# Weighting the fetched expert rows on ScalarE and adding them on VectorE in two instructions

## The reference

```python
def collect(eo, i, p, pr):
    sel = eo[i, p]                                  # two rows of 128 for each token
    return jnp.sum(pr[..., None] * sel, axis=1)     # weighted by the token's two shares
return jax.vmap(collect)(o, idx, pos, probs)
...
x = x + gb * _L1_ffn_ref(h, ...)
```

## Time and profile before

| | |
|---|---|
| median of 3 runs | 2884.38 us (2880.81 to 2885.79) |
| the profiled execution | 2883.22 us, its span 2882.0 us |
| instructions | 33776 |
| PE busy | 2172.6 us, 75% |
| DVE busy | 2227.5 us, 77% |
| ACT busy | 1554.3 us, 54% |
| POOL busy | 1204.0 us, 42% |
| TensorE's granted clock, mean | 0.878 of full |
| chain of waits, by engine | DVE 35%, PE 16%, issue 12%, ACT 9%, POOL 6% |

### The profile page before, as it was taken

The page is one execution under the profiler, slowest core; times in us unless marked ns, Lnnn a source line. Parts: engine busy times, 40 slices in busy tenths (PEclk is TensorE's granted clock), DMA queues, the critical chain, the costliest instruction groups (busy, mean ns, idle before and its releaser), DMA issues.

```text
span 2882.0 us, 33776 instructions
## 1 busy us (share of the span) xinstructions
PE 2172.6 (75%) x8767; PEld 1113.4 (39%) x8767; DVE 2227.5 (77%) x5937; ACT 1554.3 (54%) x3331; POOL 1204.0 (42%) x1166
## 2 busy tenths in 40 slices
PE   4159777988788777978878787878779787868654
PEld 2016222553244522644244522544235532444214
DVE  5874788968898688978799787978879786952371
ACT  4316824776176823885267823876157842744423
POOL 2020253715455153724555063723445154634461
PEclk7589799988998898989989899989989799989857
DMA  4001112232043312333133312323133221313223
GB/s 108 0 22 36 24 38 84 84 101 83 27 124 72 104 52 75 97 80 93 38 102 83 102 49 69 110 68 101 31 106 95 86 65 54 104 41 112 83 80 102
DMA packets 137461, 215.13 MB, mean 75 GB/s; under 512 B 17872, under 2 KB 57440, under 8 KB 134112
## 3 DMA queue, kind: packets, MB, share of 16 engines
q1 hardware_dynamic: 133088, 203.88, 25.0%
q0 software_dynamic: 4096, 8.40, 1.0%
HBM read 190.06 MB, written 22.15 MB: 74 GB/s over the span
## 4 chain that ended last, share of the span: by engine, by line
DVE 35%; PE 16%; issue 12%; ACT 9%; POOL 6%; DVEq 3%; DMA 2%; POOLq 0%; ACTq 0%; SPq 0%
DVE ps_rest L1644 6%; DVE wmask L833 6%; DVE best L975 4%; DVEq L977 3%; DVE hg L1656 3%; ACT wmask L815 3%; PE ps_rest L1385 2%; DVE z L1143 2%; POOL slots L1800 2%; PE ps_rest L1375 2%; PE ps_rest L1831 2%; PE ps_rest L1845 1%; PE ps_rest L1471 1%; DMA cols<-slots 1%; PE ps_rest L1833 1%
## 5 line engine op out<-in xcount | busy, mean ns | idle before, releaser
L1445 POOL TENSOR_TENSOR gat<-sil,cbs 128x512 f32<-128x512 f32 x256 | 325.1, 1274 | 469.8 <-ACT sil L1410 396.6
L1410 ACT ACTIVATE sil<-ps_rest,w_b1T 128x512 f32<-128x512 f32 x256 | 175.7, 686 | 471.5 <-PE ps_rest L1385 417.4
L833 DVE TENSOR_SCALAR_CACHE_REDUCE wmask<-z,tc 128x512 bf16<-128x512 f16 x512 | 349.2, 741 | 21.3 <-ACT z L800 18.1
L1009 POOL TENSOR_SCALAR wmask<-wmask 128x512 bf16<-128x512 bf16 x256 | 158.1, 617 | 341.7 <-DVE wmask L966 337.7
L1093 PE MATMUL ps_att<-z,Vp 128*32 128x128 f32 x2048 | 269.6, 277 | 16.8 <-DVE z L1165 16.8
L1385 PE MATMUL ps_rest<-rest_hT,WF 128*128 128x512 f32 x512 | 279.9, 633 | 0.0
L1375 PE MATMUL ps_rest<-gat,WP 128*128 128x512 f32 x512 | 268.7, 608 | 14.4 <-POOL gat L1445 14.4
L766 PE MATMUL ps_att<-qk 128*128 128x512 bf16 x512 | 222.6, 452 | 45.6 <-DMA qk<-bounce 21.6
L1093 PEld LDWEIGHTS ps_att<-z,Vp 128*32 128x32 f32 x2048 | 202.5, 110 | 131.3 <-issue 93.4
L1697 POOL TENSOR_TENSOR rest_c<-rest_c,hg 128x512 f32<-128x512 f32 x128 | 162.5, 1270 | 130.0 <-DVE hg L1656 129.9
L1684 POOL TENSOR_TENSOR gat<-cols,cbs 128x512 f32<-128x512 f32 x128 | 163.5, 1278 | 123.2 <-DVE cols L1565 123.2
(11 more groups left out here) (361 smaller groups left out, 4824.5 us busy)
## 6 DMA issues: line engine op xcount, KB each, us to landing
cbs<-spreads SPq DMA_DIRECT2D x128, 256.0 KB, 3.7
ccs<-spreads SPq DMA_DIRECT2D x128, 256.0 KB, 3.4
WF<-in_w SPq DMA_DIRECT2D x64, 256.0 KB, 2.7
WP<-in_w SPq DMA_DIRECT2D x64, 256.0 KB, 2.6
WF<-in_wfc SPq DMA_DIRECT2D x64, 256.0 KB, 2.7
WG<-in_wgate SPq DMA_DIRECT2D x64, 256.0 KB, 3.0
WP<-in_wproj SPq DMA_DIRECT2D x64, 256.0 KB, 3.0
qk<-bounce SPq DMA_DIRECT2D x32, 384.0 KB, 5.2
```

What stands on the lines that cost most here:

```text
L833: od.up(dve.tensor_scalar(wmask[:, i, :], z_at[i], tc[:, 0, i:i + 1], None, ALU.is_ge, ALU.add, accum_out=tc[:, 1, i:i + 1]))
L1445: weighed0.up(pool.tensor_tensor(gat[m % 2], sil[m % 2], cbs[e % 2][:], ALU.mult))
```

## The change

- `act_finish` is new: ScalarE waits for the eight fetches and for the shares, and multiplies each of the eight blocks of 128 columns of `back` by its share, in place (`ACT.Copy` with `scale` a per-partition operand). The fourth and the eighth count on a new semaphore, `shared_out`.
- `dve_finish` waits for `shared_out` twice and adds to `x` in two `tensor_tensor` instructions of 512 columns. Both count on `out1`, which has two counts per batch instead of four; between them VectorE waits for its own first.
- The planner has one thread more, `act_finishes`. The summed cost of `dve_finishes` goes from 4.96 to 1.44. All marks of all 29 threads have other values; `PERIOD` goes from -65.7 to 14.9 and `NEAR` from 0.152 to 0.243.

```diff
-PERIOD = -65.7
+PERIOD = 14.9
 TIMETABLE = {
...
-    "act_rest": (84.0600, (4864.9, 5034.0, 4871.5, 5557.9)),
+    "act_rest": (84.0600, (4455.4, 5292.9, 4111.4, 5412.5)),
...
-    "dve_finishes": (4.9600, (6158.0, 3649.8, 3263.1, 5364.1)),
+    "dve_finishes": (1.4400, (6874.3, 5480.6, 4086.7, 6120.0)),
...
+    "act_finishes": (3.6000, (7806.3, 3975.0, 3965.4, 6006.5)),
...
-    "act_attention": (76.8200, (9436.8, 7899.4, 8737.1, 13894.2)),
-    "dve_attention": (101.0400, (8189.2, 7002.3, 6134.6, 6121.7)),
+    "act_attention": (76.8200, (10505.4, 7134.6, 7634.1, 12822.5)),
+    "dve_attention": (101.0400, (8954.7, 6583.0, 5232.7, 6101.3)),
...
-    turned_back, added, out1 = sig("turned_back", 4), sig("added", 2), sig("out1", NT)
+    turned_back, added, out1 = sig("turned_back", 4), sig("added", 2), sig("out1", 2)
+    shared_out = sig("shared_out", 2)
...
     def dve_finish(b):
-        yield fetched.all(b)
-        dve.wait_ge(*fetched.all(b))
-        x = xr[b % 3]
-        for i, p in enumerate(("p1", "p2")):
-            for j in range(NT):
-                done = (od if i == 0 else out1).up(dve.scalar_tensor_tensor(x[:, j, :], back[:, i * NT + j, :], sv[p][:, j:j + 1], x[:, j, :],
-                                                                             ALU.mult, ALU.add))
-                yield 0.62
-            if i == 0:
-                od.settle()
+        x = xr[b % 3]
+        for i in range(2):
+            yield shared_out.at(b, i)
+            dve.wait_ge(*shared_out.at(b, i))
+            out1.up(dve.tensor_tensor(x[:], x[:], back[:, i * NT:(i + 1) * NT, :], ALU.add))
+            yield 0.72
+            if i == 0:
+                dve.wait_ge(*out1.at(b, 0))
+
+    def act_finish(b):
+        yield fetched.all(b)
+        act.wait_ge(*fetched.all(b))
+        yield shares.at(b)
+        act.wait_ge(*shares.at(b))
+        for i, p in enumerate(("p1", "p2")):
+            for j in range(NT):
+                done = act.activation(back[:, i * NT + j, :], back[:, i * NT + j, :], ACT.Copy, scale=sv[p][:, j:j + 1])
+                if j == NT - 1:
+                    shared_out.up(done)
+                else:
+                    oa.up(done)
+                yield 0.45
...
-    NEAR = 0.152
+    NEAR = 0.243
```

More of the change, by code:

```diff
@@ L46 @@
 FULL = (TOPK + 7) // 8
-PERIOD = -65.7
+PERIOD = 14.9
 TIMETABLE = {
-    "pe_rest": (155.6425, (4063.8, 2909.1, 2381.5, 1586.6)),
-    "act_rest": (84.0600, (4864.9, 5034.0, 4871.5, 5557.9)),
[L53 to L59, removed]
-    "dve_finishes": (4.9600, (6158.0, 3649.8, 3263.1, 5364.1)),
[L61 to L67, removed]
-    "act_attention": (76.8200, (9436.8, 7899.4, 8737.1, 13894.2)),
-    "dve_attention": (101.0400, (8189.2, 7002.3, 6134.6, 6121.7)),
[L70 to L79, removed]
@@ new lines @@
+    "pe_rest": (155.6425, (4417.8, 3623.9, 3606.2, 1766.5)),
+    "act_rest": (84.0600, (4455.4, 5292.9, 4111.4, 5412.5)),
+    "dve_rest": (96.6350, (3157.5, 6748.6, 6383.8, 4999.9)),
+    "pool_rest": (113.9225, (1737.4, 2015.9, 2844.8, 1657.8)),
+    "sp_rest": (15.3000, (7089.8, 5438.4, 6355.6, 6693.4)),
+    "pe_mixtures": (10.3100, (5846.9, 7611.3, 5250.0, 5587.3)),
+    "act_mixtures": (6.3000, (8134.6, 6365.4, 4720.0, 8578.6)),
+    "dve_mixtures": (13.5500, (5347.6, 5446.2, 5900.5, 6884.3)),
@@ new lines @@
+    "pool_mixtures": (3.9300, (8331.2, 9232.9, 12384.5, 14764.3)),
+    "dve_finishes": (1.4400, (6874.3, 5480.6, 4086.7, 6120.0)),
+    "pool_finishes": (9.0400, (3887.3, 6024.2, 5163.6, 5137.3)),
+    "act_finishes": (3.6000, (7806.3, 3975.0, 3965.4, 6006.5)),
+    "sp_finishes": (0.9000, (6856.1, 10708.9, 11455.7, 10402.6)),
+    "pe_choices": (42.2400, (1472.2, 1002.7, 2586.1, 2335.4)),
+    "act_choices": (2.5600, (10489.3, 11025.6, 11082.9, 4280.8)),
+    "dve_choices": (58.8100, (4745.6, 4518.9, 5384.4, 5070.8)),
@@ new lines @@
+    "pool_choices": (20.4800, (9372.4, 7538.3, 6851.4, 10027.2)),
+    "pe_attention": (57.4700, (7997.8, 5869.9, 5443.7, 5402.4)),
+    "act_attention": (76.8200, (10505.4, 7134.6, 7634.1, 12822.5)),
+    "dve_attention": (101.0400, (8954.7, 6583.0, 5232.7, 6101.3)),
+    "pool_attention": (6.5463, (6819.4, 6563.5, 6868.9, 8126.4)),
+    "sp_attention": (10.3500, (9501.8, 7012.5, 7718.2, 6678.1)),
+    "pe_prepares": (8.9150, (6494.4, 7059.7, 6925.8, 6588.7)),
+    "act_prepares": (3.9500, (4847.8, 5429.3, 4767.3, 0.0)),
@@ L80 @@
+    "dve_prepares": (13.8550, (11309.4, 12249.7, 11982.4, 11990.6)),
+    "pe_refills": (12.8000, (8692.6, 6412.3, 7360.2, 8369.5)),
+    "act_refills": (19.2000, (6209.8, 8412.5, 7473.7, 6238.0)),
+    "sp_rows": (0.3937, (9033.9, 8097.1, 6623.4, 7312.1)),
+    "sp_ups": (10.6875, (6668.4, 7321.3, 7935.9, 8230.1)),
+    "sp_downs": (7.0875, (7933.8, 6539.7, 5628.0, 3274.3)),
 }
@@ L2116, in dve_finishes, with act_finishes @@
             yield from dve_finish(b)
+    def act_finishes():
+        for b in every:
+            yield from act_finish(b)
     def pool_finishes():
@@ L2182, in emit @@
            ("act", "act_mixtures", act_mixtures()), ("dve", "dve_mixtures", dve_mixtures()), ("pool", "pool_mixtures", pool_mixtures()),
-           ("dve", "dve_finishes", dve_finishes()), ("pool", "pool_finishes", pool_finishes()), ("sp", "sp_finishes", sp_finishes()),
+           ("dve", "dve_finishes", dve_finishes()), ("pool", "pool_finishes", pool_finishes()), ("act", "act_finishes", act_finishes()), ("sp", "sp_finishes", sp_finishes()),
            ("pe", "pe_choices", pe_choices()), ("act", "act_choices", act_choices()), ("dve", "dve_choices", dve_choices()),
```

## The result

The changed kernel takes 2898.29 us, the median of 7 runs (2893.32 to 2915.32), against 2884.38 for the kernel before: ratio 1.006, 95% interval 1.0043 to 1.0077. It is 14 us slower; the forecast was 2872, 12 us faster. Run again later it gave 2902.68 and 1.0064 (1.0044 to 1.0084). The profiled execution took 2915.32 us, 17 above the median, so sums are made here against medians, and the profile is read for places.

The account below looks back on a forecast made before the run. VectorE's finish was taken to lie on the path, with TensorE waiting at the search's end; three quarters of 17.1 us saved, 12.8, less 0.7 for the tail gave 12 us: 2872 by the median, own range 2863 to 2880, whole 2845 to 2903.

Parts of the forecast that it names:

- What bounds the kernel: VectorE's eight finish instructions stand whole on the chain of waits, in the search in batches 0 to 4.
- Items 1 and 2: VectorE, batches 0 to 5: eight instructions removed, two additions (2.34 us) added; together 17.1 us saved after the cap.
- Item 3: ScalarE: eight multiplications of 128 columns added at 0.275 us each, 2.2 us per finish (1.3 to 3.1).
- ScalarE is on the path: Rival: multiplications fall on the chain through L815, giving back 2.2 of the 3.2 us; 2880, chance 0.14.
- the multiplications cost more than they free: Rival: VectorE's 3.3 us of waiting may simply move; +9 to +15 us over seven batches, 2896, chance 0.05.
- Item 4: The wait for the eight fetched rows moves from VectorE to ScalarE; priced at nothing.
- ScalarE waits in the wrong place: Rival: ScalarE's in-order queue stands at `fetched` with `sil` behind it; 2900, chance 0.13.
- Item 5: Tail, batch 7: multiplications and one addition take 3.0 us for 2.3, +0.7 (-0.2 to +1.6).
- Item 7: Timetable, PERIOD and NEAR: changed instruction order priced at 0; scale of 18 us over seven batches from table loads.
- Order that costs: Rival: the new order brings two table loads more per batch, -12 + 18, 2890; chance 0.12.
- The sum's last step: Of the 17.1 us saved, three quarters, 12.8 us, was taken to reach the kernel's time, less 0.7 for the tail.

Follow-up runs that it names:

- one_product: The kernel before with seven of the eight products of `dve_finish` left out: 2868.38 us, ratio 0.9949.
- products_twice: The kernel before with each of the eight products of a finish done twice in a row: 2927.67 us, ratio 1.0156.
- finish_only: The new finish in before's order on every engine; products 3/3/2 behind silus, sums late in the search or behind a MAX8: 2892.67 us, ratio 1.0024.
- order_only: The changed kernel's order with the eight old VectorE instructions in place of the two additions, nothing on ScalarE: 2905.05 us, ratio 1.0069.
- sums_alone: finish_only with six of the eight ScalarE products left out, the two sums of 512 columns kept: 2886.35 us, ratio 1.0006.
- sums_after_search: busy_6 with the two sums moved right behind `g_bad` and the products 4/4 behind two silus: 2869.33 us, ratio 0.9949.
- changed_busy: The changed kernel with 18 multiplications of zeros per Mamba head, 12 at its start and 6 ahead of x_proj: 2898.15 us, ratio 1.006.
- busy_6: finish_only with 6 multiplications of zeros on TensorE ahead of x_proj in each Mamba head: 2880.09 us, ratio 0.9991.

## Why the prediction was wrong

- **What bounds the kernel** was right: the finish lay whole on the path in the searches of batches 0 to 4 (one_product, products_twice).
- **Items 1 and 2** were right in size in the old order. The five searches end 16.3 us sooner in finish_only, for the 16.1 I had after the cap of 3.22 us by TensorE's wait. That wait shows it too: 90.7 us in 8 waits for `g_bad` before, 74.7 in 5 in finish_only, 16.0 less. The pairs that finish_only has in the searches of batches 0 and 1 took 2.36 and 2.37 us, for the 2.34 taken. For the changed kernel the items counted a saving that the order had already taken: its products would have been 2.37 us a finish, behind `g_bad` (order_only), not 5.5 in the search. The wait for `g_bad` grew there to 102.9 us in 8 waits, and to 105.4 in order_only with the old finish, so that this rise is the order's and measures nothing of the finish.
- **Item 3** was right: 64 activations at a pace of 0.293 us, for 0.275 taken; the Trainium skill's rule (ScalarE: Activation LUTs, What ACT_TABLE_LOAD costs), by which I had an estimate of 0.29, agrees with the trace. In the changed kernel the search of batch 3 has five of them in a row, 1.56 us at 1036.96, with a silu behind them; the chain of waits is on VectorE there. Leaving six of eight out of finish_only (sums_alone) gave 5 us by the ratios, but the intervals overlap, and cut by stages the six cycles are as long as in finish_only (3.8 us over before's for 3.9), with the searches ending at the same time: that ScalarE is on the path in the search isn't shown. Nor is it that the multiplications cost more than they free, by moving VectorE's waiting: 16.3 us did come free in finish_only, and with all eight sums_after_search is 15.7 us ahead.
- **Item 4 and its rival** (ScalarE waits in the wrong place, 2900): ScalarE stood 19.7 us for the fetches in 8 waits, 15.4 of them at batch 7's with nothing behind, so 4.3 in the other seven; in finish_only it was 15.4 in one wait. The time came out near that rival's 2900, but not by its mechanism: order_only has no such wait and is as slow.
- **Item 5**, the tail, was not tried by itself.
- **Item 7 is the step that failed most**: "I take 0 and put the spread in the range". The order costs 0.0069, 20 us. That this is about the 18 for which I had a scale is luck, since it isn't by table loads: there are 15 ahead of the layer 1 silu after as before. Order that costs stood at a chance of 0.12, with the finish's gain of 12 still taken off, as if the two were independent. They are not: the order moves the old finish behind `g_bad` as well, and in it the new one brings 1.4 us, not 12. By what mechanism the order costs stays open.
- **The sum's last step failed too**: "nearer to all than to nothing: three quarters". In the old order, in finish_only, 16.3 came in and 20.2 went out in the six cycles: 6.1 between `g_bad` and the last MAX8, where the late sums stand (my own placing in finish_only, not the change's), 7.9 in Mamba's head with x_proj at the lower clock, the rest in steps of 2 us or less. With the sums moved and the six multiplications ahead of x_proj, 15.7 us stay. The same six on before's own finish were not tried (18 of them cost it 4), so how much of that is the finish's isn't known; one_product, with hardly any finish and none of the six, has the same ratio, 0.9949.

## What to carry to other kernels

A change that also re-plans the order of a written-out program is two changes; price the order by running it with the old instructions before crediting or blaming the edit, and look where it puts them. A wait that is shortened moves the later blocks against TensorE's clock, and can cost them more than it brought: look at the multiplications on the chain of waits, not at the mean clock, and try a few idle ones right ahead of the block that is waited for. Where the work that is left goes matters as much as its length: in these runs it cost least in a gap of its own engine (here, behind `g_bad`), and there the old instructions, too, took 2.37 us instead of 5.5.

## What was unexpected of the hardware

The same eight multiplications on the path took 3.70 us in one batch and up to 6.7 in another, by the granted clock over them, and before and finish_only, with the same order on TensorE, differ by 9.5 us in their sum. Twelve idle multiplications 15 us ahead didn't help them, six right ahead did (592 ns against 1061 in the median). And changed_busy, with a mean clock of 0.887, is 0.7% slower than busy_6 with 0.875 (ratios 1.006 and 0.9991): the mean doesn't tell the time. A pair of additions of 0.69 us each took 1.41 us in six of eight finishes of the changed kernel and 2.52 where GpSimd was multiplying (sums_after_search, batch 0's finish).
